# Graph attention layer in fp32 halves: DMA transposes issued ahead of a step's second weight tile, and third parts of the values as 64-column products at the end of the batch

## The chip, the cores and the metric

One core of a Trainium2 chip. The metric is the device time of one execution, in microseconds (us). The kernel before is given as the median of 3 runs; the trace is from one further execution, profiled, whose own time stands beside its span below. Engines: TensorE (PE), VectorE (DVE), ScalarE (ACT), GpSimd (POOL) and SyncE (SP), which only issues DMAs here.

## What is computed

```python
q = x @ wq.T + bq;  k = x @ wk.T + bk;  v = x @ wv.T + bv            # x: 384 x 1024
q2 = (q @ wiq.T + biq).reshape(N, H, D).transpose(1, 0, 2)           # H = 16 heads, D = 64
k2, v2 = ...                                                         # the same with wik, wiv
scores = jnp.einsum('hnd,hmd->hnm', q2, k2) * scale + mask[None]     # mask 384 x 384, from 6144 edges
attn = jax.nn.softmax(scores, axis=-1)
out = jnp.einsum('hnm,hmd->hnd', attn, v2)
out = out.transpose(1, 0, 2).reshape(N, OUT_F) @ wo.T + bo
return _layernorm(x + out, axis=-1)
```

## The kernel before

It is written with explicit semaphores: every engine has a queue of its own, in the order of the code, and an instruction that waits holds all that stands behind it in that queue. All fp32 products are made of a high part (rounded to the short fp32 format) and a low part (the rest): hi x hi, hi x lo, lo x hi.

Weights come as 56 tiles of 128 x 1024 (512 KB): 24 for q, k and v, 8 for the inner v, then two for each of the 8 pairs of heads (q and k), and 8 for the output projection. SP loads each into one of 4 slots of `w_raw` (`load_tile`, L241 to 249). A load waits until ScalarE and VectorE or GpSimd have split the tile that was in its slot, four tiles earlier. ScalarE makes the high part (L443), VectorE the low part of the early tiles, GpSimd (L352) that of the tiles from the second pair on.

From tile `PAIR_TILE` on, the work goes in steps, one for each pair of heads. In step j:
- TensorE multiplies half of the q tile of pair j, does the scores of pair j-1 (L999, 18 products of 64 rows), the other half of the q tile, the values of pair j-2 (L1018), and then the k tile of pair j.
- VectorE masks the six score blocks of pair j-1 (L810: places 0 to 2 are head 0, 3 to 5 head 1), then makes the low planes of the probabilities (L830), evacuates q of pair j (L785), adds up the values of pair j-2 (L797) and evacuates k (L785). The first mask of each head waits for the lo transpose of that head of the pair before, since the low planes lie where the scores go.
- ScalarE splits the two weight tiles of the next step, makes the exps (L526) and the high planes (L538), and evacuates q, the halves of the values, and k.
- GpSimd makes the low part of the next step's first tile, the parts of `vp` (the values of two heads in three bf16 parts), waits until all six low planes of pair j-1 are done, and then makes the low part of the second tile.
- SP turns the planes of pair j-1: four DMA transposes, hi and lo of head 0, hi and lo of head 1 (`turn`, L293 to 304). Each waits for its planes, the first for the values of pair j-2 too, whose input is overwritten. Its place in SP's queue is between two weight loads and is set by the line `a, odd = divmod(t - PAIR_TILE - 2 * RING - 1, 2)`.

The values of a pair are out[head] = vp x turned planes, over three blocks m of 128 keys. `vp` has 192 columns for each head: the first and second bf16 part (`two`, 128 columns) and the third (`low`, 64 columns). Each block has six products: `two` x hi for both heads, `low` x hi for both, `two` x lo for both. The output of head h is bank 2 or 4; its partitions 0 to 63 and 64 to 127 are two halves of a sum, which ScalarE and VectorE add. `low` goes onto partitions 0 to 63 for both heads.

After the last step come the output projections (L925), with the scores and values of pair 7 and the values of pair 6 between them, and then the layer norm and the stores.

Of the kernel before, what the change touches and what calls it, by code (L numbers as in the profile page):

```python
# [17 lines left out]
N = 384  # L18
NT = N // P
# [3 lines left out]
D = F // HEADS  # L23
PAIRS = HEADS // 2
# [14 lines left out]
RING = 4  # L39
L1_TILES = 3 * KT  # L40
IV_TILE = L1_TILES
PAIR_TILE = IV_TILE + KT
# [25 lines left out]
def gnn_layer(nc, start, x_rows, weights, bias_cols, bias_rows, edge_weights, edge_cols, edge_rows,  # L68
              key_rows, mask_cells, out):
    with ExitStack() as ctx:  # L70
        def sb(name, shape, dt):
            return ctx.enter_context(nc.sbuf_tensor(name, shape, dt))

        def sem(name):
            return ctx.enter_context(nc.semaphore(name))
# [24 lines left out]
        vp = sb("vp", [P, 2, NT, 2, 3 * D], BF16)  # L100
# [21 lines left out]
        turned_hi, turned_lo = (p.rearrange("p (h b m q) -> p h b m q", h=2, b=NT, m=NT) for p in planes[1:])  # L122
# [53 lines left out]
        out_bank = [bank[i] for i in (2, 4)]  # L176
# [5 lines left out]
        def v_part(par, z):  # L182
# [31 lines left out]
        vp_hi_done, vp_done = sem("vp_hi_done"), sem("vp_done")  # L214
        scores_seen = sem("scores_seen")
        scores_ready, masked, exp_done = (sem(n) for n in ("scores_ready", "masked", "exp_done"))
        pv_done = sem("pv_done")
# [3 lines left out]
        turned_hi_landed, turned_lo_landed = (  # L221
            [sem(f"{n}{h}") for h in range(2)] for n in ("turned_hi_landed", "turned_lo_landed"))
        half_done, sum_done = sem("half_done"), sem("sum_done")
# [13 lines left out]
        def _(sp):  # L237
# [3 lines left out]
            def load_tile(t, s):  # L241

                sp.wait_ge(w_hi_done, t - RING + 1)
                if t - RING >= POOL_TILE:
                    sp.wait_ge(w_lo_pool, t - RING + 1 - POOL_TILE)
                else:
                    sp.wait_ge(w_lo_dve, t - RING + 1)
                sp.dma_start(w_raw[:, s, :], weights[ds(t, 1), :, :].rearrange("a p n -> (a p) n"))\  # L248
                  .then_inc(raw_loaded[s], 16)

            def load_rows(g, slot):
                sp.dma_start(keyb[:, slot, :], key_rows[ds(g, 1), :].to_broadcast([P, GE]))\
                  .then_inc(rows_loaded, 16)
# [39 lines left out]
            def turn(a, h):  # L293
                if a:

                    sp.wait_ge(pv_done, NT * a)
                sp.wait_ge(plane_hi_done, 2 * NT * a + NT * (h + 1))
                sp.dma_start_transpose(turned_hi[:, h, :, :, :].rearrange("p b m q -> p (b m) q"),  # L298
                                       plane_hi[:, h, :, :].rearrange("p b n -> p (b n)"))\
                  .then_inc(turned_hi_landed[h], 16)  # L300
                sp.wait_ge(plane_lo_done, 2 * NT * a + NT * (h + 1))
                sp.dma_start_transpose(turned_lo[:, h, :, :, :].rearrange("p b m q -> p (b m) q"),  # L302
                                       plane_lo[h].rearrange("p b n -> p (b n)"))\
                  .then_inc(turned_lo_landed[h], 16)

            for t in range(2 * RING, TILES):
                load_tile(t, t % RING)
                g, s = divmod(t, RING)
                if s == 1 and g < GROUPS:

                    sp.wait_ge(rows_loaded, 16 * g)
                    sp.wait_ge(cells_ready, g - 1)
                    load_rows(g, g % 2)
                if t == IV_TILE + RING + LEAD:

                    sp.wait_ge(cells_ready, GROUPS)
                    sp.dma_start(res[:, :, :], x_rows).then_inc(res_loaded, 16)
                    sp.dma_start(bo_row, bias_rows[1:2, :].to_broadcast([P, F])).then_inc(bo_loaded, 16)
                if t == RING * GROUPS - 1:
                    sp.dma_start(row[:, :], bias_rows[0:1, :].to_broadcast([P, F])).then_inc(biv_loaded, 16)  # L320
                a, odd = divmod(t - PAIR_TILE - 2 * RING - 1, 2)
                if a >= 0 and not odd:
                    for h in range(2):
                        turn(a, h)
# [580 lines left out]
        def _(pe):  # L905
            def tile_ready(t, pair_tile=False):

                if pair_tile and not (isinstance(t, int) and t < POOL_TILE):
                    pe.wait_ge(w_lo_pool, t + 1 - POOL_TILE)
                else:  # L910
                    pe.wait_ge(w_lo_dve, t + 1)

            def by_outputs(out_ps, s, k, moving_hi, moving_lo):

                cols = slice(k * P, (k + 1) * P)
                pe.matmul(out_ps, w_hi[:, s, cols], moving_hi, start=(k == 0), stop=False)  # L916
                pe.matmul(out_ps, w_hi[:, s, cols], moving_lo, start=False, stop=False)  # L917
                return pe.matmul(out_ps, w_lo[:, s, cols], moving_hi, start=False, stop=(k == KT - 1))  # L918
# [17 lines left out]
            for k in range(KT):  # L936
                cols = slice(k * P, (k + 1) * P)
# [38 lines left out]
            for k in range(KT):  # L976
                t = IV_TILE + k
# [5 lines left out]
                for n in range(NT):  # L983
                    cols = slice(n * P, (n + 1) * P)
# [16 lines left out]
                            if left is q_lo:  # L1001
                                ins.then_inc(scores_ready, 1)

            def values(a, par, m):
                if m == 0:

                    pe.wait_ge(vp_done, a + 1)
                    if isinstance(a, int) and a == PAIRS - 1:
                        pe.wait_ge(sum_done, 2 * a)
                    else:  # L1010

                        pe.wait_ge(masked, 2 * NT * a + 3 * NT)
                    for h in range(2):
                        pe.wait_ge(turned_hi_landed[h], 16 * a + 16)
                        pe.wait_ge(turned_lo_landed[h], 16 * a + 16)

                def product(h, cols, turned, start=False, stop=False):
                    return pe.matmul(out_bank[h][0:cols.stop - cols.start, 0:N].rearrange("p (b q) -> p b q", b=NT),  # L1018
                                     vp[:, par, m, h, cols], turned[:, h, :, m, :], start=start, stop=stop)


                two, low = slice(0, 2 * D), slice(2 * D, 3 * D)
                for h in range(2):
                    product(h, two, turned_hi, start=(m == 0))
                for h in range(2):
                    product(h, low, turned_hi)
                for h in range(2):
                    ins = product(h, two, turned_lo, stop=(m == NT - 1))
                ins.then_inc(pv_done, 1)

            def step(j, par):
                start = isinstance(j, int) and j < 1
                more = not (isinstance(j, int) and j < 2)
                a = j - 1
                t = PAIR_TILE + 2 * j
                for which in range(2):
                    tile_ready(t + which, pair_tile=True)

                    pe.wait_ge(acc_free, L1_TILES + 2 * j + (which + 1))
                    for k in range(KT):  # L1040
                        ins = by_outputs(acc[which][:, 0:N], 2 * par + which, k, h_hi[:, which * KT + k, :],
                                         h_lo[:, which * KT + k, :])
                        if k == KT - 1:
                            ins.then_inc(tile_done, 1)
                        if start:
                            continue
                        if which == 0 and k == SCORE_PLACE:


                            pe.wait_ge(acc_free, L1_TILES + 2 + 2 * j)  # L1050
                            if isinstance(a, int) and a == 0:

                                pe.wait_ge(v2_ready, 2 * NT)
                            scores(a, 1 - par)
                    if which == 0 and more:
                        for m in range(NT):
                            values(j - 2, par, m)

            step(0, 0)
            step(1, 1)  # L1060
# [6 lines left out]
            def project(n, k, pieces=slice(None)):  # L1067
                if n == 0:

                    tile_ready(WO_TILE + k, pair_tile=True)  # L1070

                    pe.wait_ge(att_lo_done, k + 2)
                cols = slice(n * P, (n + 1) * P)
                return by_nodes(OUT_PIECES[n][pieces], WO_TILE + k, att_hi[:, k, cols], att_lo[:, k, cols],
                                k == 0, k == KT - 1)

            a = PAIRS - 1
# [7 lines left out]
            scores(a, 1)  # L1085
            project(0, 0, right)
            project(0, 1, right)
            for m in range(NT):
                values(a - 1, 0, m)
            project(0, 2)  # L1090


# [6 lines left out]
            pe.wait_ge(masked, 2 * NT * PAIRS)  # L1099
            for k in range(4):  # L1100
                project(2, k, left)
            for m in range(NT):
                values(a, 1, m)
            for k in range(4, KT - 1):
                project(0, k)
                project(1, k)
# [58 lines left out]
```

## Time and profile before

| | |
|---|---|
| median of 3 runs | 332.25 us (331.42 to 334.98) |
| the profiled execution, its own time | 332.98 us |
| its span | 330.9 us |
| TensorE matmul busy | 291.9 us, 88% |
| VectorE, ScalarE, GpSimd busy | 176.4, 162.6 and 146.9 us |
| value products L1018 | 144, mean 410 ns |
| mean granted TensorE clock | 0.955 of full speed |

A row of the timeline or of the chain begins with the start and the duration in us. A bracket at its end is the idle time of the engine before it and what ended that. A granted clock of 1.00 is 2.4 GHz, and 0.5 is 1.2 GHz. A matmul's recorded duration is about twice the distance to the next start, since matmuls are pipelined; the distances between starts are what counts. Two products on different rows of the array, as the scores of two heads, stand in one row as x2. Many of ScalarE's and VectorE's rows overlap the next by 0.1 us for the same reason.

### The profile page before, as it was taken

The numbers are of one execution on the slowest core, as the hardware profiler recorded it, in microseconds if no ns is written. First come the engines' busy times: TensorE is split into PE (matmuls) and PEld (weight loads), VectorE is DVE, ScalarE is ACT, GpSimd is POOL, SyncE is SP. The second block draws the span as 40 slices with busy tenths as digits, with TensorE's granted clock in tenths as the row PEclk, the third lists the DMA queues.
The fourth block names the chain that finished last, engine by engine and source line by source line (L and its number), as shares of the span: only waits on it lengthen the run. The fifth ranks groups of instructions, "written<-read, shape, count | busy, mean of one in ns | idle before, by whom it ended". The sixth has DMA issues, their size and how long they took to land.

```text
span 330.9 us, 5094 instructions
## 1 busy us (share of the span) xinstructions
PE 291.9 (88%) x1578; PEld 248.8 (75%) x1578; DVE 176.4 (53%) x434; ACT 162.6 (49%) x304; POOL 146.9 (44%) x130
## 2 busy tenths in 40 slices
PE   6999999999999999999829696896979495998991
PEld 6999999999999888899707575392859364384880
DVE  4889866666666522616336282625546272701065
ACT  4953333333333442219537584846659375851123
POOL 2002446464655455596622718072464527094100
PEclk9999999999999999999969999796999989699998
DMA  7877753646533794513290917356290909172013
GB/s 276 313 266 260 218 187 129 190 127 182 193 119 130 269 343 136 150 51 129 71 200 0 234 38 183 86 129 140 71 198 12 255 3 208 63 163 45 0 43 149
DMA packets 51918, 49.27 MB, mean 149 GB/s; under 512 B 41056, under 2 KB 41920, under 8 KB 51776
## 3 DMA queue, kind: packets, MB, share of 16 engines
q1 hardware_dynamic: 49792, 47.63, 49.6%
q0 software_dynamic: 1680, 0.62, 1.0%
q10 hardware_dynamic: 432, 0.85, 0.7%
q8 instruction: 7, 0.11, 0.1%
q14 instruction: 7, 0.06, 0.0%
HBM read 37.44 MB, written 2.21 MB: 120 GB/s over the span
## 4 chain that ended last, share of the span: by engine, by line
SPq 12%; DVE 9%; DMA 8%; PE 7%; POOL 6%; ACT 5%; issue 5%; DVEq 0%; POOLq 0%; ACTq 0%
DMA scratch<-shared 8%; SPq L298 7%; POOL w_lo L352 5%; SPq L302 5%; DVE shared L830 4%; PE bank L925 4%; PE bank L1018 3%; ACT shared L526 2%; ACT scratch L538 2%; DVE stats L890 1%; DVE res L889 1%; DVE shared L810 1%; SPq L248 1%; ACT h_hi L443 1%; DVE row_inv L819 0%
## 5 line engine op out<-in xcount | busy, mean ns | idle before, releaser
L389 POOL DMA_INDIRECT mask_cells<-scratch x48 | 56.4, 1175 | 72.9 <-DMA mask_cells<-scratch 30.0
L352 POOL TENSOR_TENSOR w_lo<-w_raw,w_hi 128x1024 fp32r<-128x1024 f32 x18 | 43.1, 2398 | 70.8 <-DVE shared L830 69.2
L1018 PE MATMUL bank<-scratch,vp 128*128 128x384 f16 (+1 forms) x144 | 39.6, 410 | 28.2 <-DMA scratch<-shared 28.2
L443 ACT ACTIVATE w_hi<-w_raw 128x1024 fp32r<-128x1024 f32 x49 | 51.5, 1053 | 21.2 <-PE bank L925 19.6
L916 PE MATMUL bank<-x_hi,w_hi 128*128 128x384 f32 x176 | 58.8, 334 | 0.0
L917 PE MATMUL bank<-x_lo,w_hi 128*128 128x384 f32 x176 | 58.8, 334 | 0.0
L918 PE MATMUL bank<-x_hi,w_lo 128*128 128x384 f32 x176 | 58.8, 334 | 0.0
L1018 PEld LDWEIGHTS bank<-scratch,vp 128*128 128x128 bf16 (+1 forms) x144 | 11.7, 114 | 55.8 <-issue 54.8
L810 DVE CUSTOM_DVE_ANT_0 shared<-bank,mask 128x384 f32<-128x384 f32 x48 | 24.8, 555 | 52.7 <-DMA scratch<-shared 48.1
L526 ACT ACTIVATE shared<-shared,neg_max 128x384 f32<-128x384 f32 x48 | 29.0, 604 | 37.0 <-DVE neg_max L810 37.0
L641 DVE TENSOR_TENSOR w_lo<-w_raw,w_hi 128x1024 fp32r<-128x1024 f32 x31 | 37.8, 1223 | 16.2 <-ACT w_hi L443 15.2
L916 PE MATMUL bank<-h_hi,w_hi 128*128 128x384 f32 x128 | 44.4, 347 | 0.0
L918 PE MATMUL bank<-h_hi,w_lo 128*128 128x384 f32 x128 | 42.9, 335 | 0.0
L917 PE MATMUL bank<-h_lo,w_hi 128*128 128x384 f32 x128 | 42.8, 334 | 0.0
L486 ACT ACTIVATE h_hi<-bank,bcol 128x384 f32 (+1 forms) x24 | 14.0, 582 | 56.7 <-PE bank L918 56.7
L916 PEld LDWEIGHTS bank<-x_hi,w_hi 128*128 128x128 f32 x176 | 33.0, 188 | 0.0
L917 PEld LDWEIGHTS bank<-x_lo,w_hi 128*128 128x128 f32 x176 | 33.0, 188 | 0.0
L918 PEld LDWEIGHTS bank<-x_hi,w_lo 128*128 128x128 f32 x176 | 33.0, 188 | 0.0
L830 DVE SCALAR_TENSOR_TENSOR shared<-shared,row_inv,scratch 128x384 f16<-128x384 f32 x48 | 29.0, 617 | 6.0 <-ACT scratch L538 5.5
L538 ACT ACTIVATE scratch<-shared,row_inv 128x384 f16<-128x384 f32 x48 | 27.5, 605 | 0.9 <-DVEq L820 0.2
L723 DVE SCALAR_TENSOR_TENSOR h_lo<-bank,bcol,h_hi 128x384 f32 (+1 forms) x24 | 14.8, 617 | 24.3 <-ACT h_hi L486 23.5
L916 PEld LDWEIGHTS bank<-h_hi,w_hi 128*128 128x128 f32 x128 | 24.0, 188 | 2.2 <-issue 1.8
(100 smaller groups left out, 462.9 us busy)
## 6 DMA issues: line engine op xcount, KB each, us to landing
w_raw<-weights SPq DMA_DIRECT2D x53, 512.0 KB
shared<-key_rows SPq DMA_DIRECT2D x6, 512.0 KB
shared<-start SPq DMA_DIRECT2D x5, 320.0 KB, 7.0
res<-x_rows SPq DMA_DIRECT2D x1, 1536.0 KB, 6.9
out<-res SPq DMA_DIRECT2D x6, 256.0 KB, 2.0
mask_cells<-scratch POOLq DMA_INDIRECT x48
shared<-start ACTq DMA_DIRECT2D x2, 320.0 KB, 6.2
mask_cells<-mask SPq DMA_DIRECT2D x1, 576.0 KB, 4.9
```

Source lines behind the costliest of these rows:

```text
L352: nc.gpsimd.tensor_tensor(lo, w_raw[:, s, cols], hi.bitcast(F32), ALU.subtract)\
L389: nc.gpsimd.indirect_dma_start(out=mask_cells, out_offset=bass.IndirectOffsetOnAxis(ap=cell[:, c:c + 1], axis=0), in_=cell_value[:, c:c + ...
L443: nc.scalar.activation(w_part(t, s, slice(0, F))[0], w_raw[:, s, :], ACT.Copy).then_inc(w_hi_done, 1)
L526: nc.scalar.activation(probs[:, place, :], probs[:, place, :], ACT.Exp, bias=neg_max[:, place:place + 1], scale=-1.0, accum_out=row_sum[:, ...
L538: nc.scalar.activation(plane_hi[:, h, b, :], probs[:, place, :], ACT.Copy, scale=row_inv[:, place:place + 1]).then_inc(plane_hi_done, 1)
L641: nc.vector.tensor_tensor(lo, w_raw[:, s, cols], hi.bitcast(F32), ALU.subtract)\
L810: nc.vector.tensor_tensor_reduce(out=probs[:, place, :], in0=score_bank[i][:, 0:N], in1=mask[:, i // 2, :], scale=-SCALE, scalar=3.0e38, o ...
L830: nc.vector.scalar_tensor_tensor(out=plane_lo[h][:, b, :], in0=probs[:, place, :], scalar=row_inv[:, place:place + 1], in1=plane_hi[:, h, ...
L916: pe.matmul(out_ps, w_hi[:, s, cols], moving_hi, start=(k == 0), stop=False)
L917: pe.matmul(out_ps, w_hi[:, s, cols], moving_lo, start=False, stop=False)
L918: return pe.matmul(out_ps, w_lo[:, s, cols], moving_hi, start=False, stop=(k == KT - 1))
L1018: return pe.matmul(out_bank[h][0:cols.stop - cols.start, 0:N].rearrange("p (b q) -> p b q", b=NT), vp[:, par, m, h, cols], turned[:, h, :, ...
```

## The change

The transposes of pair a now stand in SP's queue ahead of the load of the second weight tile of their step, and not behind it. The order of the products in `values` changes, and so does where the third parts go: the 12 products of 128 columns come first, then the six of 64 columns, block by block, those of head 1 onto partitions 64 to 127. `pv_done` is counted up in that last loop.

```diff
-                a, odd = divmod(t - PAIR_TILE - 2 * RING - 1, 2)
+                a, odd = divmod(t - PAIR_TILE - 2 * RING, 2)
                 if a >= 0 and not odd:
                     for h in range(2):
                         turn(a, h)
...
-                def product(h, cols, turned, start=False, stop=False):
-                    return pe.matmul(out_bank[h][0:cols.stop - cols.start, 0:N].rearrange("p (b q) -> p b q", b=NT),
-                                     vp[:, par, m, h, cols], turned[:, h, :, m, :], start=start, stop=stop)
+                def product(h, m, cols, turned, **flags):
+                    first = h * D if cols.start else 0
+                    rows = slice(first, first + cols.stop - cols.start)
+                    return pe.matmul(out_bank[h][rows, 0:N].rearrange("p (b q) -> p b q", b=NT),
+                                     vp[:, par, m, h, cols], turned[:, h, :, m, :], **flags)
...
                 two, low = slice(0, 2 * D), slice(2 * D, 3 * D)
-                for h in range(2):
-                    product(h, two, turned_hi, start=(m == 0))
-                for h in range(2):
-                    product(h, low, turned_hi)
-                for h in range(2):
-                    ins = product(h, two, turned_lo, stop=(m == NT - 1))
-                ins.then_inc(pv_done, 1)
+                for m in range(NT):
+                    for h in range(2):
+                        product(h, m, two, turned_hi, start=(m == 0), stop=False)
+                    for h in range(2):
+                        product(h, m, two, turned_lo, start=False, stop=(m == NT - 1))
+                for m in range(NT):
+                    for h in range(2):
+                        ins = product(h, m, low, turned_hi, start=False, stop=True, skip_group_check=True)
+                    ins.then_inc(pv_done, 1)
```

The same `values(a, par)` is called once for a pair where `values(a, par, m)` was called for m = 0, 1, 2. Its waits are those that stood at m = 0.

On SP, around the first and the last turn (L248 is a weight load, L298 a hi and L302 a lo transpose, L332 the stores of the output). Between these two places both kernels have two loads and four transposes in turn:

```order
-L248 DMA w_raw<-weights 128x1024 [waits w_lo_pool,w_hi_done] x4
+L248 DMA w_raw<-weights 128x1024 [waits w_lo_pool,w_hi_done] x3
 L298 DMA_TRANSPOSE scratch<-scratch 128x9x128 [waits plane_hi_done]
 L302 DMA_TRANSPOSE scratch<-shared 128x9x128 [waits plane_lo_done]
@@ -68,4 +68,5 @@
 L298 DMA_TRANSPOSE scratch<-scratch 128x9x128 [waits plane_hi_done,pv_done]
 L302 DMA_TRANSPOSE scratch<-shared 128x9x128 [waits plane_lo_done]
+L248 DMA w_raw<-weights 128x1024 [waits w_lo_pool,w_hi_done]
```

Each turn moved past one load: the first stands behind three loads of the last kind, where it stood behind four, and the load that was ahead of the last turn is now behind it.

On TensorE, the value batch of a step (L1018; 128x384 and 64x384 are the outputs, two heads in one row):

```order
-L1018 MATMUL bank<-scratch,vp 128x384 x2
-L1018 MATMUL bank<-scratch,vp 64x384 x2
-L1018 MATMUL bank<-scratch,vp 128x384 x4
-L1018 MATMUL bank<-scratch,vp 64x384 x2
-L1018 MATMUL bank<-scratch,vp 128x384 x4
-L1018 MATMUL bank<-scratch,vp 64x384 x2
-L1018 MATMUL bank<-scratch,vp 128x384 x2
+L1018 MATMUL bank<-scratch,vp 128x384 x12
+L1018 MATMUL bank<-scratch,vp 64x384 x6
```

The number of products is the same, 12 and 6; the three pairs of 64 columns stood among the others and now stand together behind them.

## Rows read from the trace of the kernel before

**Rows 1.** Sums of waits: engine, line, waited for: us in total, times, longest us.

```profile
POOL w_lo L352 <- DVE shared L830: 69.2, 8, 11.2
...
DVE shared L810 <- DMA scratch<-shared: 48.1, 14, 8.1
...
PE bank L1018 <- DMA scratch<-shared: 28.2, 8, 7.0
```

**Rows 2.** The waits of SP's DMA queue alone, the longest.

```profile
SPq L245 <- POOL w_lo L352: 104.1, 11, 11.5
```

**Rows 3.** The chain that ended last, one step: start us, us, what.

```profile
255.43 1.29 SPq L298
...
260.18 3.34 DMA scratch<-shared
...
270.79 2.40 POOL w_lo L352
273.67 1.25 SPq L298
```

**Rows 4.** Timeline of ScalarE and then VectorE, 251 to 271 us.

```profile
251.31 0.56 ACT L503 ACTIVATE h_hi<-bank,bcol 128x384 fp32r<-128x384 f32 x1
...
253.45 0.58 ACT L503 ACTIVATE h_hi<-bank,bcol 128x384 fp32r<-128x384 f32 x1 [0.56 <-PE bank L918]
...
255.85 1.05 ACT L443 ACTIVATE w_hi<-w_raw 128x1024 fp32r<-128x1024 f32 x1
261.69 0.61 ACT L526 ACTIVATE shared<-shared,neg_max 128x384 f32<-128x384 f32 x1 [4.79 <-DVE neg_max L810]
...
264.38 0.61 ACT L526 ACTIVATE shared<-shared,neg_max 128x384 f32<-128x384 f32 x1 [0.79 <-DVE neg_max L810]
...
267.42 2.24 ACT L538 ACTIVATE scratch<-shared,row_inv 128x384 f16<-128x384 f32 x4
269.57 0.56 ACT L503 ACTIVATE h_hi<-bank,bcol 128x384 fp32r<-128x384 f32 x1
...
261.09 0.56 DVE L810 CUSTOM_DVE_ANT_0 shared<-bank,mask 128x384 f32<-128x384 f32 x1 [6.28 <-DMA scratch<-shared]
...
263.78 0.56 DVE L810 CUSTOM_DVE_ANT_0 shared<-bank,mask 128x384 f32<-128x384 f32 x1 [1.17 <-DMA scratch<-shared]
...
270.53 0.61 DVE L785 SCALAR_TENSOR_TENSOR h_lo<-bank,bcol,h_hi 128x384 fp32r<-128x384 f32 x1
```

**Rows 5.** Timeline of TensorE: the score batches of pairs 0 and 1.

```profile
149.83 0.44 PE L999 MATMUL bank<-h_hi 64*128 64x384 f32 x2
...
160.45 0.45 PE L999 MATMUL bank<-h_hi 64*128 64x384 f32 x2 [0.25 <-DVE h_lo L785]
...
162.24 0.44 PE L916 MATMUL bank<-h_hi,w_hi 128*128 128x384 f32 x1
```

**Rows 6.** Timeline of TensorE: value batches of pairs 0, 1, 6 and 7.

```profile
171.60 5.21 PE L1018 MATMUL bank<-scratch,vp 128*128 128x384 f16 x18 [7.01 <-DMA scratch<-shared]
...
189.87 3.76 PE L1018 MATMUL bank<-scratch,vp 128*128 128x384 f16 x18 [2.75 <-DMA scratch<-shared]
193.33 0.47 PE L916 MATMUL bank<-h_hi,w_hi 128*128 128x384 f32 x1
...
281.97 6.24 PE L1018 MATMUL bank<-scratch,vp 128*128 128x384 f16 x18 [3.86 <-DMA scratch<-shared]
...
300.32 3.76 PE L1018 MATMUL bank<-scratch,vp 128*128 128x384 f16 x18 [1.19 <-DMA scratch<-shared]
```

**Rows 7.** Timeline of TensorE's weight loads in the value batch of pair 4.

```profile
245.81 0.14 PEld L1018 LDWEIGHTS bank<-scratch,vp 128*64 128x64 bf16 x2 [0.32 <-issue]
246.25 0.44 PEld L1018 LDWEIGHTS bank<-scratch,vp 128*128 128x128 bf16 x4 [0.31 <-issue]
247.00 0.14 PEld L1018 LDWEIGHTS bank<-scratch,vp 128*64 128x64 bf16 x2 [0.32 <-issue]
```

**Rows 8.** Timeline of ScalarE: the last four hi planes of pair 0.

```profile
156.68 2.23 ACT L538 ACTIVATE scratch<-shared,row_inv 128x384 f16<-128x384 f32 x4
```

More of the change, by code:

```diff
@@ L1002, in scores @@
                                 ins.then_inc(scores_ready, 1)
[L1004 to L1012, printed above, removed]
-                    for h in range(2):
-                        pe.wait_ge(turned_hi_landed[h], 16 * a + 16)
-                        pe.wait_ge(turned_lo_landed[h], 16 * a + 16)
-                def product(h, cols, turned, start=False, stop=False):
-                    return pe.matmul(out_bank[h][0:cols.stop - cols.start, 0:N].rearrange("p (b q) -> p b q", b=NT),
-                                     vp[:, par, m, h, cols], turned[:, h, :, m, :], start=start, stop=stop)
-                two, low = slice(0, 2 * D), slice(2 * D, 3 * D)
-                for h in range(2):
-                    product(h, two, turned_hi, start=(m == 0))
-                for h in range(2):
-                    product(h, low, turned_hi)
-                for h in range(2):
-                    ins = product(h, two, turned_lo, stop=(m == NT - 1))
-                ins.then_inc(pv_done, 1)
@@ new lines, in values @@
+            def values(a, par):
+                pe.wait_ge(vp_done, a + 1)
+                if isinstance(a, int) and a == PAIRS - 1:
+                    pe.wait_ge(sum_done, 2 * a)
+                else:
+                    pe.wait_ge(masked, 2 * NT * a + 3 * NT)
+                for h in range(2):
+                    pe.wait_ge(turned_hi_landed[h], 16 * a + 16)
+                    pe.wait_ge(turned_lo_landed[h], 16 * a + 16)
+                def product(h, m, cols, turned, **flags):
[3 more added lines that the diff above has]
+                                     vp[:, par, m, h, cols], turned[:, h, :, m, :], **flags)
+                two, low = slice(0, 2 * D), slice(2 * D, 3 * D)
+                for m in range(NT):
+                    for h in range(2):
+                        product(h, m, two, turned_hi, start=(m == 0), stop=False)
[5 more added lines that the diff above has]
+                    ins.then_inc(pv_done, 1)
@@ L1055, in step @@
                     if which == 0 and more:
-                        for m in range(NT):
-                            values(j - 2, par, m)
+                        values(j - 2, par)
             step(0, 0)
@@ L1087, in _ @@
             project(0, 1, right)
-            for m in range(NT):
-                values(a - 1, 0, m)
+            values(a - 1, 0)
             project(0, 2)
@@ L1101, in _ @@
                 project(2, k, left)
-            for m in range(NT):
-                values(a, 1, m)
+            values(a, 1)
             for k in range(4, KT - 1):
```

## The prediction

> **What bounds the kernel now.** I read the page first: TensorE is busy for 88% of the span, but its row of tenths falls from 9 to 6, 7 and 4 in the second half, and the chain that ended last spends little on its projections. So the half with attention is held by something else. The sums of waits say what [rows 1]: GpSimd waits 8 times for the last low plane; VectorE and TensorE wait 48.1 and 28.2 us for the lo transposes. SP's own waits [rows 2] show 104.1 us in front of a weight load (L245), for GpSimd's low parts. The chain [rows 3] joins them into a ring that goes round once a step: the transposes of one pair (first start 255.43, last landing 260.18 + 3.34 = 263.5), the softmax of the next pair, GpSimd's low part of the step's second tile (270.79, 2.4 us), its slot's load, and the next transposes at 273.67. The timeline of the step [rows 4] gives the inside: mask place 0 starts at 261.09, when head 0's lo transpose has landed; place 3 at 263.78, when head 1's has; the last four hi planes begin at 267.42; VectorE is through with the lo planes at 270.53, and GpSimd starts. The value batches [rows 6] start at 171.60 for pair 0, 281.97 for pair 6 and 300.32 for pair 7: 128.7 us for seven rounds, 18.4 us each. The transposes need nothing of that low part. They only stand behind its load in SP's queue.
>
> **The transposes ahead of the load.** Let S be the start of a pair's first transpose, now 273.67. It needs the third hi plane of head 0, ready at 267.42 + 0.6 = 268.0, and the end of the previous pair's values: landing 263.5 + 3.46 at full clock (189.87 to 193.33) [rows 6] = 267.0. So S could be near 268.05, 5.6 us earlier. The third lo plane follows within 0.7, inside the 1.3 us that the hi transpose takes to issue; head 1's planes are ready likewise ahead of theirs.
>
> The ring then: S to the last landing 8.1 us [rows 3], landing to the next third hi plane 268.0 - 263.5 = 4.5: 12.7 us in place of 18.4. In those 8.1 the 512 KB weight tile still runs ahead of the transposes in the same queue. Behind them it costs them nothing, so 8.1 is the late end; four issues of 1.3 and 1.5 for data, an estimate, give 6.7 as the early one.
>
> The weight load moves behind four issues, some 6 us. It fills a ring slot that is read two steps later, 26 us even in the new round; a load lands in about 4 (an estimate from the transposes' 3.34): hidden. Uncovered, if its tile were wanted within the round, it would cost these 6 a round. Behind it in SP's queue stands the load of the next step's first tile, which waits for a later low part anyway, and then the next transposes, which come 5 us after that.
>
> **What is the bound then: TensorE.** From one score batch to the next with no values between them: 149.83 to 160.45 [rows 5], less 0.25 idle, 10.4 us at 2.4 GHz. With values of 3.46 that is 13.8, more than the ring's 12.7. So the second part of the change counts in full.
>
> **The value batch.** By its weight loads at full clock [rows 7]: two 64-column ones and a change of shape take 0.44, four of 128 and a change 0.75. So a product is 0.155 and a change 0.13. Before, 18 products and six changes; after, 12 products, then six low ones, two changes. If the two heads' low products, whose outputs now lie in partitions 0 to 63 and 64 to 127, run together: 15 x 0.155 + 0.26 = 2.6 us. If in a line: 3.05. No row has column halves side by side; the nearest are the scores, 18 products of 64 rows in pairs, 160.45 to 162.24 [rows 5]: 0.1 each, two thirds of 0.155 although they stream fp32. I take 2.6.
> The Trainium skill (TensorEngine Tiling, Tiling Modes) says that a change of tiling mode drains the engine. By the 0.13 us of the rows, four changes fewer are 0.5 of the 0.85 saved. If no drain went with the order, the batch would be 3.1 and the sum 4 us higher.
>
> **The new round.** TensorE 10.4 + 2.6 = 13.0 us. The others fit, tightly [rows 4]. ScalarE from its first exp to the q evacuation: 269.57 - 261.69 = 7.9, less a wait of 0.8; from the q evacuation to the end of the second weight split: 255.85 + 1.0 - 251.31, less a wait of 0.56, 5.0: together 12.1. VectorE takes 270.53 - 261.09, less its 1.17 and with ScalarE's chain 0.4 more, 8.7 from the first mask to the q evacuation, and frees TensorE's accumulator 9.3 after it. TensorE is back there when scores 1.8, half a tile 2.1 (a quarter of 10.4 - 1.8), values 2.6 and a tile 4.3 are done, counted from the scores, which begin 1.1 before the masks: 9.7. The slack is 0.4, hence 0.3 a round for waits, as the 0.25 before 160.45: **13.3**. The value batches no longer follow idle time of TensorE (7.01 before 171.60; the batch at 281.97 took 6.24 at 1.2 GHz), so the full clock is in the 13.0 already.
>
> **The sum**, on the profiled execution. Pair 0's third hi plane is ready at 156.68 + 0.6 [rows 8]; S is 157.3. Landing at 164.0 to 165.4; TensorE ready at 160.45 + 1.8 + 2.1 = 164.3; values at 165.0. In the first round softmax still waits for the landing, so the accumulator comes 0.8 late. Five rounds of 13.3: 66.5. Pairs 5 to 7, with output projections in place of tiles: scores of pair 7 at 2.6 + 4.3 + 1.5 (evacuation) = 8.4 after pair 5's values, values of pair 6 3.1 later; from there 300.32 - 281.97, less the idle 1.19 and the slow batch's 5.9 - 2.6, 13.8; and 1.1 for the low part behind pair 7's planes (8.4 + 1.1 + 8.7 + 2.4 = 20.6, where TensorE is at 19.6). Together 26.4. After the last values 330.9 - 300.32, less 0.8: 29.8. 165.0 + 0.8 + 66.5 + 26.4 + 29.8 = 288.5 us of span. Outside the span lie 332.98 - 330.9 = 2.1; the median lies 0.7 below this execution: **290 us**, 42 below.
>
> **The rivals.**
> TensorE bound, as summed: 0.62. Low products in a line add 8 x 0.45: 294. Early landings and no waits: 286. Its own range is 285 to 297.
> The ring of transposes stays the bound: TensorE idles before the values, runs them at 1.2 GHz (15 x 0.31 + 0.3 = 5 us), and the next S waits for their end: 8.1 + 5 + 0.6 = 13.7, with idle 14.3 a round. For it: the clock was down in such batches. [...] 165 + 7 x 14.3 + 30.6 = 296; with the ends 293 to 302: 0.20.
> Another wait takes most of it: softmax engines that rested in every round now run all the time, and the late accumulator repeats and grows to 3 us, 16 a round: 165 + 112 + 31 + 1.4 = 309: 0.12. Against: masks take 0.56 with transposes in flight too.
> Slower: SP sits in the turn's waits, a slot is refilled late and its split stalls. From S to that tile's use runs a chain of issue 6, load 4, split 1 and low part 2.4, projection 4.3, evacuation 1.3, softmax 9: 28 us, spread over four rounds, 7 each. It decides from loads that take about 45 us more; at 18.8 a round the time is 335. For it: the queue is in order. Against: that slack. 0.03. No change, because the turn's own waits end only where the load's did: against it stand the 5.6 us; 0.03, 332.
>
> The range, 284 to 305, reaches from under the first case's early end to within the third's. Over 1% is about what a measurement of this kernel can tell from no change: faster by it 0.94, within 0.03, slower 0.03.
>
> **What would show it.** Right: a pair's first transpose within 0.3 us of its third hi plane's end, ahead of L352 in that step; value batches 13.0 to 13.6 apart, 2.6 long, low products starting in twos; idle before L1018 under 5 us in all; granted clock 1.00 from 160 on; 29.8 us after the last values. Wrong: batches 14 or more apart with a named wait (DMA before L1018: the second rival; L785 before L916: the third); splits that wait for w_raw: the fourth; low products 0.155 apart: in a line.

## The result, and the profile after

The changed kernel takes 289.63 us (median of 4 runs, 288.81 to 291.41), the kernel before 332.91: a ratio of 0.870, 95% interval 0.864 to 0.877. The forecast was 290. Timed again beside the experiments it took 289.21 (ratio 0.871, 0.869 to 0.873). Its profiled execution took 290.02 us with a span of 288.0.

The page after; first the busy time of the engines:

```profile
PE 276.0 (96%) x1578; PEld 248.2 (86%) x1578; DVE 180.6 (63%) x434; ACT 161.7 (56%) x304; POOL 147.6 (51%) x130
...
PE   8999999999999999999999889999999999999990
...
PEclk9999999999999999999999999999999999999996
```

TensorE's row of tenths has no holes left in the second half, and the clock stays up until the last slice.

The waits after, to be held against [rows 1, 2]:

```profile
POOL w_lo L352 <- DVE shared L830: 35.8, 8, 5.9
...
DVE shared L810 <- PE bank L999: 13.1, 8, 2.1
...
DVE shared L810 <- DMA scratch<-shared: 1.8, 1, 1.8
```

VectorE's masks waited 48.1 us for transposes; now it is 1.8, and they wait for TensorE's scores. TensorE waits for a transpose once, 1.1 us. The value batches, the lines that answer to [rows 6] (TensorE's timeline; 18 products in one row, and the product that follows them; of the first batch only the start of the row is shown):

```profile
164.52 0.65 PE L1018 MATMUL bank<-scratch,vp 128*128 128x384 f16 x3 [1.08 <-DMA scratch<-shared]
...
178.95 2.73 PE L1018 MATMUL bank<-scratch,vp 128*128 128x384 f16 x18
181.61 0.44 PE L916 MATMUL bank<-h_hi,w_hi 128*128 128x384 f32 x1
...
192.02 2.73 PE L1018 MATMUL bank<-scratch,vp 128*128 128x384 f16 x18
...
205.09 2.73 PE L1018 MATMUL bank<-scratch,vp 128*128 128x384 f16 x18
...
243.71 2.73 PE L1018 MATMUL bank<-scratch,vp 128*128 128x384 f16 x18
...
258.19 2.73 PE L1018 MATMUL bank<-scratch,vp 128*128 128x384 f16 x18
```

From start to start the rounds are 13.07 us (178.95, 192.02, 205.09, and the same to 231.24), where they were 18.4. A batch is 181.61 - 178.95 = 2.66 us. SP's queue shows the new order, the four transposes of a pair and then the two loads:

```profile
195.15 1.31 SPq L298 DMA_TRANSPOSE scratch<-scratch  x1
196.51 1.37 SPq L302 DMA_TRANSPOSE scratch<-shared  x1
197.97 1.36 SPq L298 DMA_TRANSPOSE scratch<-scratch  x1
199.39 1.38 SPq L302 DMA_TRANSPOSE scratch<-shared  x1
200.86 3.40 SPq L248 DMA_DIRECT2D w_raw<-weights  x2
```

The third hi plane and GpSimd's low part, for which the load waits, in the same step (timelines of ScalarE and GpSimd):

```profile
194.48 2.23 ACT L538 ACTIVATE scratch<-shared,row_inv 128x384 f16<-128x384 f32 x4
```

```profile
197.83 2.40 POOL L352 TENSOR_TENSOR w_lo<-w_raw,w_hi 128x1024 fp32r<-128x1024 f32 x1 [4.22 <-DVE shared L830]
```

The first transpose starts at 195.15, right behind the third hi plane (the first of the four that begin at 194.48, 0.6 us long), and before the low part at 197.83.

### The profile page after: what moved, and what is told of

Its sections match the earlier page's. It is cut to its first block, busy times and chain, and to the rows that moved or that the text cites. A ratio compares the mean times of both kernels' runs of the same rounds, so it can differ in the third digit from the quotient of the medians.

```text
span 288.0 us, 5094 instructions
## 1 busy us (share of the span) xinstructions
PE 276.0 (96%) x1578; PEld 248.2 (86%) x1578; DVE 180.6 (63%) x434; ACT 161.7 (56%) x304; POOL 147.6 (51%) x130
## 4 chain that ended last, share of the span: by engine, by line
PE 79%; DVE 8%; ACT 6%; issue 2%; POOL 2%; DMA 1%; SPq 1%; DVEq 0%; ACTq 0%; POOLq 0%
PE bank L925 18%; PE bank L916 17%; PE bank L918 16%; PE bank L917 16%; PE bank L1018 4%; PE bank L999 4%; PE bank L941 3%; DVE shared L830 3%; ACT shared L526 3%; ACT scratch L538 2%; POOL w_lo L352 2%; DVE stats L890 2%; PE bank L934 1%; DMA scratch<-shared 1%; DVE res L889 1%
## 5 line engine op out<-in xcount | busy, mean ns | idle before, releaser
L352 POOL TENSOR_TENSOR w_lo<-w_raw,w_hi 128x1024 fp32r<-128x1024 f32 x18 | 43.2, 2405 | 37.6 <-DVE shared L830 35.8
L916 PE MATMUL bank<-x_hi,w_hi 128*128 128x384 f32 x176 | 58.8, 334 | 0.0
L916 PE MATMUL bank<-h_hi,w_hi 128*128 128x384 f32 x128 | 44.3, 346 | 1.1 <-DVE h_lo L785 1.1
L810 DVE CUSTOM_DVE_ANT_0 shared<-bank,mask 128x384 f32<-128x384 f32 x48 | 25.0, 556 | 17.9 <-PE bank L999 13.1
L830 DVE SCALAR_TENSOR_TENSOR shared<-shared,row_inv,scratch 128x384 f16<-128x384 f32 x48 | 31.1, 660 | 4.1 <-ACT scratch L538 2.9
L916 PEld LDWEIGHTS bank<-x_hi,w_hi 128*128 128x128 f32 x176 | 33.0, 188 | 0.0
L916 PEld LDWEIGHTS bank<-h_hi,w_hi 128*128 128x128 f32 x128 | 24.0, 188 | 5.0 <-issue 3.6
L705 DVE SCALAR_TENSOR_TENSOR res<-shared,scratch,res 128x512 uint8<-128x512 bf16 (+7 forms) x48 | 25.7, 546 | 0.0
L917 PEld LDWEIGHTS bank<-h_lo,w_hi 128*128 128x128 f32 x128 | 24.0, 188 | 0.0
```

Of the source, the lines that this page charges most:

```text
L352: nc.gpsimd.tensor_tensor(lo, w_raw[:, s, cols], hi.bitcast(F32), ALU.subtract)\
L705: nc.vector.scalar_tensor_tensor(out=unread[:, c, 0:n], in0=keyb[:, slot, P * c:P * c + n].rearrange("p a e -> p (a e)"), scalar=key[:, ds ...
L830: nc.vector.scalar_tensor_tensor(out=plane_lo[h][:, b, :], in0=probs[:, place, :], scalar=row_inv[:, place:place + 1], in1=plane_hi[:, h, ...
```

## The experiments

Each kernel is the changed one with one edit, unless its text says otherwise. All ratios are to the kernel before, timed beside them on the same chip (332.6 us).

**The turn alone.** The kernel before with only `a, odd = divmod(t - PAIR_TILE - 2 * RING, 2)`.

> The kernel before, with the turn moved and the value products as they were. If TensorE bounds the new round (theory): a value batch takes 3.46 us where the changed kernel's takes 2.65, so a round is 13.07 + 0.81 = 13.9 us, pairs 1 to 5 lie 13.9 apart, eight batches cost 6.5 us more than in the changed kernel, and the time is 296 us. If softmax or the transposes bound the round (rival), the longer batch hides in TensorE's idle time and the time is that of the changed kernel, 290 us. If both parts of the change were needed for the gain (rival), it stays above 310.

Measured: 294.55 us, ratio 0.888 (0.882 to 0.893). Two value batches:

```profile
192.83 3.77 PE L1018 MATMUL bank<-scratch,vp 128*128 128x384 f16 x18
196.30 0.47 PE L916 MATMUL bank<-h_hi,w_hi 128*128 128x384 f32 x1
...
206.76 3.77 PE L1018 MATMUL bank<-scratch,vp 128*128 128x384 f16 x18
```

A batch of 3.47 us and a round of 13.93: in each steady round the 0.8 us come back in full. The theory holds: 38 of the 43 us are the turn's, the other 5 are the batch's, because TensorE bounds the round.

The total was 1.5 us below the expected 296, which had counted the longer batch eight times. The trace has it in the four rounds from pair 1 to 5 and after the last values. Pair 0 to pair 1 takes 14.41 us, where the changed kernel has 14.43: there the longer batch fills TensorE's wait for VectorE's L785 (0.21 us left of 1.08). Pair 5 to 7 takes 27.42 where the changed kernel has 26.95: its two waits of 0.5 us for low parts are gone. The two kernels below that take the second part apart missed their expected totals, by 2.0 and 3.2 us, in the same direction and in part for the same reason.

**The products alone.** The turn is back behind the load.

> The changed kernel with the turn put back behind the load. Theory: the ring of low part, load issue, transposes and softmax bounds the round at 18.4 us as before, TensorE has over 4 us of idle time in it, and the shorter batch shows only after pair 7's values (0.8 us): 332 us, 0 to 1 below the kernel before, with batches after long idle still at 1.2 GHz and about 5 us long. Rival, that the shorter batch brings each round forward by its own 0.8 us: 326 us.

Measured: 333.06 us, ratio 1.002 (0.998 to 1.005). The batches lie 18.1 to 18.6 us apart and still follow idle time, 7.2 us at most:

```profile
170.33 5.10 PE L1018 MATMUL bank<-scratch,vp 128*128 128x384 f16 x18 [7.23 <-DMA scratch<-shared]
...
206.78 4.34 PE L1018 MATMUL bank<-scratch,vp 128*128 128x384 f16 x18 [3.55 <-DMA scratch<-shared]
```

Alone, the second part of the change is worth nothing that can be measured. It only counts behind the first.

**The third parts in a line, and the old order with them side by side.** Two kernels that take the second part apart:

```diff
-                    first = h * D if cols.start else 0
+                    first = 0
```

> The changed kernel, but the third parts of both heads go onto partitions 0 to 63 (order unchanged). Theory: the six products then stream one after another, 6 x 0.16 in place of 3 x 0.16, so a batch takes 3.1 us in place of 2.65, a round 13.5, and the time is 290 + 8 x 0.45 = 293.5 us. Rival, that what was saved is the changes of shape alone: batch 2.65 still, 290 us.

```diff
                     for h in range(2):
                         product(h, m, two, turned_hi, start=(m == 0), stop=False)
+                    for h in range(2):
+                        product(h, m, low, turned_hi, start=False, stop=False, skip_group_check=True)
                     for h in range(2):
-                        product(h, m, two, turned_lo, start=False, stop=(m == NT - 1))
-                for m in range(NT):
-                    for h in range(2):
-                        ins = product(h, m, low, turned_hi, start=False, stop=True, skip_group_check=True)
+                        ins = product(h, m, two, turned_lo, start=False, stop=(m == NT - 1))
                     ins.then_inc(pv_done, 1)
```

> The changed kernel with the third parts of the two heads side by side, but each block's pair back between its 128-column products (six changes of shape in place of two). Theory: a change costs 0.13 us, four more are 0.52, so a batch takes 3.1 to 3.2 us, a round 13.6, and the time is 290 + 8 x 0.5 = 294 us. Rival, that only the pairing saved time: 2.65 us and 290 us.

Measured: 291.52 and 290.81 us, both 0.877 (0.874 to 0.880 and 0.873 to 0.881). The first kernel's batch, and under it the second's, each with the product that ends it and the next batch:

```profile
193.12 3.22 PE L1018 MATMUL bank<-scratch,vp 128*128 128x384 f16 x18
196.27 0.44 PE L916 MATMUL bank<-h_hi,w_hi 128*128 128x384 f32 x1
...
206.69 3.22 PE L1018 MATMUL bank<-scratch,vp 128*128 128x384 f16 x18
```

```profile
191.12 3.30 PE L1018 MATMUL bank<-scratch,vp 128*128 128x384 f16 x18
194.11 0.47 PE L916 MATMUL bank<-h_hi,w_hi 128*128 128x384 f32 x1
...
204.57 3.30 PE L1018 MATMUL bank<-scratch,vp 128*128 128x384 f16 x18
```

With the turn alone and the changed kernel these make four batches, measured from their first product to the start of L916 behind them:

| | six changes of shape | two |
|---|---|---|
| third parts in a line | 3.47 us | 3.15 us |
| side by side | 2.99 us | 2.66 us |

Side by side saves 0.48 or 0.49 us, which is three products of 0.16: two column halves do stream at once. The order saves 0.32 or 0.33 in the table, but the table is not quite fair to it: L916 starts 0.03 us behind a product of 128 columns, with which the batches of six changes end, and 0.26 behind one of 64. The rounds, which are free of that, are 13.93, 13.57, 13.45 and 13.07, each its batch + 10.41 to 10.46. In them the order saves 0.36 or 0.38 us for four changes, so a change costs 0.09 us, not 0.13. TensorE's timeline agrees: starts lie 0.16 us apart within one width and 0.26 where the width changes. The two effects add up. The totals scatter by about 1 us against that, as the first half of the kernel does from run to run.

**The turn three loads further ahead.** The turn then stands ahead of four weight loads, in place of one, that the kernel before has in front of it.

```diff
-                a, odd = divmod(t - PAIR_TILE - 2 * RING, 2)
-                if a >= 0 and not odd:
+                a, odd = divmod(t - PAIR_TILE - 2 * RING + 3, 2)
+                if 0 <= a < PAIRS and not odd:
```

> The changed kernel with each turn three loads further ahead in SP's queue, so that four weight loads of 512 KB stand behind it. By the sum's view, a load has a slack of far more than its 4 us of landing: even these tiles are split 12 us after the turn was issued, so nothing changes, 290 us within 1, rounds 13.07. By the rival of the prediction that a slot refilled late stalls its split: ScalarE waits for w_raw in each round, and a round takes 1 us or more longer, 298 us and above.

Measured: 323.04 us, ratio 0.972 (0.970 to 0.974). The expectation was wrong and the rival right. SP's queue and ScalarE's timeline in one step:

```profile
195.52 1.49 SPq L302 DMA_TRANSPOSE scratch<-shared  x1
197.10 1.01 SPq L248 DMA_DIRECT2D w_raw<-weights  x2
```

```profile
195.59 0.52 ACT L516 ACTIVATE x_hi<-att_sum 128x384 f32 x1 [0.57 <-DVE att_sum L797]
201.03 1.06 ACT L443 ACTIVATE w_hi<-w_raw 128x1024 fp32r<-128x1024 f32 x1 [4.92 <-DMA w_raw<-weights]
```

The load is issued at 197.10, lands 3.9 us later, and ScalarE's split stood waiting since 196.1 (195.59 + 0.52). Behind the split in ScalarE's queue are the exps of the next softmax, so the whole ring stops with it: rounds of 15 to 20 us. I had placed the split one round too late: the splits of a step stand ahead of that step's softmax, not behind it.

**The turn one load further ahead.** To test that corrected view; `+ 1` in place of `+ 3` above.

> The changed kernel with the turn one load further ahead, so that both loads of a step stand behind it. Corrected view after the kernel with three loads further (323 us, where a load was issued only when its split was due): the first of these two tiles is split 12 us after the turn has been issued and a load lands in 4, so nothing changes: rounds 13.07, 289 us. If a load behind the turn stalls its split in any place (rival), ScalarE waits for w_raw in each round: 295 us or more.

Measured: 289.50 us, ratio 0.871 (0.869 to 0.873), rounds of 13.07. So both loads of a step can stand behind the turn, and four cannot. Three were not run.

**GpSimd's low part without its wait for the planes.** In every step (`pool.wait_ge(plane_lo_done, ...)` taken out in both places), and only after the last step.

> The changed kernel without GpSimd's wait for the six low planes ahead of the second tile's low part, in every step and at the end (nothing of its data depends on that wait). In the changed kernel VectorE's L830 takes 0.84 us in place of 0.62 where GpSimd's L371 runs beside it. If that is contention of the two engines, L830 is slowed here by L352 too, for 2.4 us of each step: planes up to 1 us later, against about 0.7 us of slack of the accumulator, rounds 13.1 to 13.5, time 290 to 293 us in spite of TensorE's two waits of 0.5 us for low parts at the end, which go. If there is no contention: rounds 13.07 and 289 us.

> The same wait taken away only after the last step, ahead of the low part of tile WO+3. TensorE waited 0.5 us for it before the output projections with this tile (252.60). That wait goes: 0.5 us less, 289.5 us; if contention slows pair 7's planes, its transposes come up to 1 us later, which TensorE's 14.5 us of work before pair 7's values hides in part: 289.5 to 290.5 us.

Measured: 296.56 us (0.892, 0.890 to 0.894) and 288.20 us (0.867, 0.865 to 0.869). In the first kernel VectorE's low planes (there L828), with GpSimd's L371 and L352:

```profile
194.68 3.99 DVE L828 SCALAR_TENSOR_TENSOR shared<-shared,row_inv,scratch 128x384 f16<-128x384 f32 x2
```

```profile
194.66 0.92 POOL L371 TENSOR_TENSOR vp<-v_rest,vp 128x384 bf16<-128x384 f32 x1
195.54 2.71 POOL L352 TENSOR_TENSOR w_lo<-w_raw,w_hi 128x1024 fp32r<-128x1024 f32 x1
```

Two planes that take 1.15 us took 3.99. VectorE's instructions and GpSimd's take turns: the first plane ends 0.42 us after the end of L371, the second 0.42 us after the end of L352. This is so in every second round; in the others it is the small product L816 (L818 of the changed kernel) that is held, 2.35 us. The rounds grow to 14.67. I expected some slowing, up to 1 us, and 290 to 293 us; the slowing was 2.8 and the time outside that range.

At the end, where no further round follows, it pays, by more than the 0.5 us at best that I had expected. The wait before 252.60 is gone. Two planes of pair 7 are held there too (3.72 us from 244.34), but TensorE has other work meanwhile. Pair 7's values come 13.68 us after pair 6's (242.80 to 256.48) in place of 14.51 (242.64 to 257.15 in the changed kernel timed beside it). This is the fastest kernel here that leaves nothing out, 1.0 us below the changed one.

**GpSimd's low parts first.** Both low parts of a step in a row, `v_low` behind the wait for the planes.

```diff
+                low_part(t + LEAD + 1, s0 + 1)
                 if not (isinstance(j, int) and j < 1):
-                    v_low(j - 1, 1 - par)
-
                     pool.wait_ge(plane_lo_done, 2 * NT * j)
-                low_part(t + LEAD + 1, s0 + 1)
+                    v_low(j - 1, 1 - par)
```

The same was done after the last step.

> The changed kernel with GpSimd's two low parts of a step one after the other, and the parts of vp behind the wait for the low planes. Nothing of GpSimd then runs beside L830, so L830 takes 0.62 us throughout (it took up to 4 us for two where GpSimd ran); the low parts at the end come before TensorE wants them, so its two waits of 0.5 us go; rounds stay at 13.07, since TensorE bounds them: 288.2 us, 1.0 below the changed kernel. Rival: vp's third part, now 3 us after the planes, comes too late for the values, which then wait: above 290 us.

Measured: 291.29 us, ratio 0.876 (0.874 to 0.878): slower by 2 and above 290, as the rival had it, but not for the rival's reason: no value batch after pair 0's waits. GpSimd's two low parts, 4.73 us in a row, now run beside the softmax and hold VectorE. VectorE's and GpSimd's timelines (L829 and L817 there are the L830 and L818 of the changed kernel):

```profile
179.82 2.30 DVE L829 SCALAR_TENSOR_TENSOR shared<-shared,row_inv,scratch 128x384 f16<-128x384 f32 x2
...
191.71 2.12 DVE L817 TENSOR_TENSOR row_inv<-row_sum,downs 128x3 f32<-128x3 f32 x1
```

```profile
176.32 4.73 POOL L352 TENSOR_TENSOR w_lo<-w_raw,w_hi 128x1024 fp32r<-128x1024 f32 x2
...
189.09 4.73 POOL L352 TENSOR_TENSOR w_lo<-w_raw,w_hi 128x1024 fp32r<-128x1024 f32 x2
```

In every second round two planes take 2.30 us for 1.15, and that is still hidden: the round stays at 13.07 or 13.08. In the others a product of 128 x 3 numbers takes 2.12 us, until GpSimd's low parts end, and TensorE waits 0.95 us for the accumulator: 14.3 in place of 13.07.

**The same order of GpSimd's work, in the kernel before.** SP's queue and the value products are as they were.

> The kernel before, with SP's order and the value products as they were, and only GpSimd's order changed as in the kernel just above, so that the low part for which the load in front of the turn waits is done before the softmax is. If it was this wait in SP's queue that held the transposes (theory), they start with the planes: rounds of 13.9 us as with the turn moved alone, 294 us. If what counted was that the load's 512 KB run ahead of the transposes, or anything else in that order (rival), rounds stay well above 15: more than 305 us.

Measured: 296.10 us, ratio 0.891 (0.888 to 0.893), steady rounds of 13.9 to 14.5 us. SP's queue in one step, the loads of the step still in front of the turn:

```profile
206.65 2.65 SPq L248 DMA_DIRECT2D w_raw<-weights  x2
212.11 1.29 SPq L298 DMA_TRANSPOSE scratch<-scratch  x1
```

The order in SP's queue was never touched, only the moment at which the load in front of the turn may go. So it was the wait of that load which held the transposes, not its bytes. The rounds above 13.93 are those in which VectorE's small product is held again, here for up to 2.25 us.

**Without the third parts.** The six products are left out of each batch.

> The changed kernel without the third bf16 parts' six products in each value batch (left out; the values lose their last bits). A batch takes 1.85 us in place of 2.66. If TensorE is the only bound of the new round (theory), a round is 10.41 + 1.85 = 12.3 us and the time 289.2 - 8 x 0.8 = 282.8 us. If the softmax engines bound it just as tightly, the accumulator's evacuation L785 shows as a wait before L916 in each round and a round stays at 12.6 to 13.07: 285 to 289 us.

Measured: 286.89 us, ratio 0.865 (0.861 to 0.868). The time lies in the second case's range, 285 to 289, and 4 us above the first case's. The rounds take 12.53 to 12.75 for a batch of 1.83, where TensorE alone would need 12.24. In the steady rounds the first product of the second tile now starts up to 0.51 us after the one before it, where 0.17 is usual, and the wait named there is for VectorE's L785:

```profile
222.07 0.44 PE L916 MATMUL bank<-h_hi,w_hi 128*128 128x384 f32 x1 [0.17 <-DVE h_lo L785]
```

So TensorE bounds the changed kernel's round, but the softmax stands only 0.3 to 0.5 us behind it.

## Why the prediction was right

**What bound the kernel.** The ring with the load in SP's queue is confirmed from two sides, by moving the turn and by ending the load's wait earlier without moving it.

**The terms of the sum.**

| term | forecast | measured |
|---|---|---|
| values of pair 0 | 165.0 | 164.52 |
| pair 0 to pair 1 | 14.1 | 14.43 |
| four rounds, pair 1 to 5 | 53.2 | 52.29 |
| pair 5 to pair 7 | 26.4 | 26.95 |
| after pair 7's values start | 29.8 | 29.81 |
| span | 288.5 | 288.0 |

The sum came out by terms that are nearly right and whose errors partly cancel. Pair 0's values: this execution was 1.15 us early by the first scores already (148.68, where they stood at 149.83 [rows 5]), so against them they were 0.7 late. The step that failed there is the landing. I gave the four transposes 6.7 to 8.1 us from first issue to last landing, without the 512 KB in front of them; for pair 0 it took 8.2 (156.16 to 164.39), more than my late end. For pairs 1 to 6 it took 7.5 to 7.8 (195.15 to 202.7 for the lines shown above, the last landing 3.3 us after its issue), where the kernel before has 8.1 to 8.7. So the load in front had cost some 0.6 us, not the 1.5 of my early end. This did no more harm because the turn is now early enough.

The rounds: 10.41 + 2.66 = 13.07, without any of the 0.3 that I had added for waits. The slack of the accumulator was real and sufficed. In the batch the pairing was right and the change of shape too dear, 0.13 for 0.09 us; with 0.155 for a product that is 0.163, the batch came out nearly the same, 2.6 for 2.66. The rows could have warned me: by these prices the old batch would take 18 x 0.155 + 6 x 0.13 = 3.57 us, and it took 3.46.

The first round was 1.36 us longer than the others, I had 0.8: TensorE idles 1.08 us before L916 for the late evacuation, as said. The last two lost 0.5 us twice, waiting for a low part (I had 1.1 once). Pair 5 to 6 took 12.47 us where the sum has 11.5, and pair 6 to 7 14.48 where it has 14.9: errors that partly cancel again.

**The load behind the turn.** Here a step was wrong although its result was right. I gave the moved load 26 us until its tile is read, two rounds. With the turn three loads further ahead, the first load behind it was wanted 1.0 us before it was even issued. The moved load's tile stands three tiles, one and a half steps, further on: some 14 us after its issue, 10 after landing. The rival *slower* was priced too far away by the same mistake. I had a late load spread over four rounds, needing 45 us to decide. In fact a split that waits holds the softmax behind it in ScalarE's queue at once, and a load some 10 us later would have done (an estimate from the slack just given). That mechanism costs 34 us in the kernel with the turn three loads further ahead.

**The rivals.** TensorE waited for transposes only before pair 0's values, and the granted clock was 1.00 (2.4 GHz) in all the batches, so the ring did not remain the bound. The engines of the softmax did get in each other's way, though not by what I named: VectorE's L830 was held by GpSimd's L371 once in each of the four steady rounds, for about half a microsecond, hidden behind TensorE:

```profile
193.02 1.68 DVE L830 SCALAR_TENSOR_TENSOR shared<-shared,row_inv,scratch 128x384 f16<-128x384 f32 x2
```

```profile
192.69 0.92 POOL L371 TENSOR_TENSOR vp<-v_rest,vp 128x384 bf16<-128x384 f32 x1
```

In the kernel before, no instruction of GpSimd ran beside L830, so its trace could not show this: L830 took 0.61 or 0.62 us in all 48 cases.

## What to carry to other kernels

Look in each in-order queue for an instruction that waits for something late in front of one that has long been ready; here the transposes stood ready for 5.6 us a round behind a load that nobody needed soon. When the ring is broken, sum the next engine's work per round before pricing a second edit: the shorter value batch is worth 5 us behind the first edit and nothing without it. And before moving a load back, count its slack at the head of the queue that reads it, with everything that stands behind that reader.

## What was not expected of the hardware

**VectorE and GpSimd lock each other out.** Held were VectorE's L830 (two planes 3.99 us for 1.15, in the kernel without the wait) and L818 (2.12 us for about 0.15, in the kernel with the low parts first), each with both tensors in SBUF. The masks L810 and the evacuations L785, with one input in PSUM, took their 0.56 and 0.61 us beside the same GpSimd instruction. GpSimd is held too: in the kernel without the wait L371 took 1.34 us for 0.92 in some rounds, and L352 2.71 for 2.40. The Trainium skill says this (SBUF — State Buffer, Who interferes with whom): a VectorE instruction with two SBUF inputs contends with a GpSimd instruction that reads SBUF. It also calls the ports that the two share an exclusive lock. The trace agrees, and by that rule the kernel with the low parts first could have been foreseen to be slowed.

**Four DMA transposes between SBUF and SBUF take 7.5 us** from first issue to last landing in steady rounds (7.5 to 7.8), with no weight load right in front; with one 0.4 us in front of them, as in the kernel before, they take 8.1 to 8.7. Pairs 0 and 7 of the changed kernel took 8.2 and 8.3 without a load in front; why is not shown. The DMA engines of the changed kernel while only the transposes of pair 0 are under way (the last two columns are their share and GB/s), and in a microsecond with weight loads alone:

```profile
158.00:159.00 1.00, 1.00 (x6) 0.72 (x5) 0.96 (x3) 1.00 (x2) 0.21 (x1) 1.00 1.08 197
159.00:160.00 1.00, 0.75 (x9) 0.71 (x10) 0.24 (x1) 1.00 (x3) 1.00 (x1) 1.00 1.11 211
...
166.00:167.00 1.00, 1.00 (x10) 0.43 (x8) 0.59 (x3) 0.31 (x1) 0.37 (x1) 1.00 0.80 324
```

With transposes they are full, at about 200 GB/s. Loads alone moved 324 GB/s at a share of 0.80, but in the microsecond before only 197.

**Two products on the two column halves of TensorE stream at once** when their outputs lie in partitions 0 to 63 and 64 to 127: 0.16 us for both, their starts less than 0.01 us apart. On the same partitions they take 0.16 each. A change between 128 and 64 columns costs 0.09 us.
